# A graph layer's edge pass on one core: gathers issued ahead, scatters one pair closer, eight degree products and the inverse roots moved to its end

## The chip, the cores and the metric

The kernel runs on 1 core of one Trainium2 chip. The time is device microseconds of one execution, as a median over runs; the trace comes from one execution taken by the hardware profiler. PE is TensorE, DVE is VectorE, ACT is ScalarE, POOL is GpSimd, and SP issues DMAs only.

## The reference

Two layers over 50,000 nodes with 256 features and 12,500 edges sorted by destination. In the first layer h is the relu of the layer norm of x; each edge gathers the rows of its two ends, normalises them, projects them to q, k and v, forms a message and adds it to the row of its destination. The second layer is a weighted, symmetrically normalised graph convolution (with self loops) and a two-layer head.

```python
h = jnp.maximum(_layernorm(x), 0.0)
# first layer, per edge
dk = silu(edge_attr @ Wdk.T + bdk); dv = silu(edge_attr @ Wdv.T + bdv)
attn = silu(jnp.sum(q[dst] * k[src] * dk, axis=1)) * cosine_cutoff(edge_weight)
msg = v[src] * dv * attn[:, None]
agg = segment_sum(msg, dst, N)
x = x + h + agg @ Wo.T + bo
# second layer, h taken anew from x; row = src, col = dst
deg = segment_sum(edge_weight, row, N) + 1.0
dinv = where(deg > 0, rsqrt(deg), 0.0)
h7 = segment_sum((h @ W)[col_sl] * norm[:, None], row_sl, N) + b   # norm = dinv[row] * ew * dinv[col]
x = x + relu(h7 @ W1 + b1) @ W2 + b2
```

## The kernel before

The edges lie in 98 columns of 128 (`EC`), two columns to a pair, so 49 pairs (`EP`). There are three stages.

**Edge pass of the first layer (the function `messages` of each engine, steps 0 to 55).** Each engine has its own instruction list, written out in the order of steps; step s works on several pairs at once, each at another lag. At step s POOL gathers the four blocks of pair s (rows of x, 128 x 256 each: two by source into `XS`, a ring of two pairs, two by destination into `kept`, which has a place for every column; both count into `m_x`), DVE takes the statistics of pair s-1, ACT makes its relu, POOL takes the inverse roots of pair s-2 (`power`), and PE projects pair s-4 (`project`), merges the messages of pair s-5 by destination and multiplies those of pair s-6 by Wo. ACT copies that product out at step k+7 for pair k, and POOL adds it to the table `sums0` in DRAM (`scatter_add`) at step k+9 (`SCATTER_LAG`), after a wait for the scatter of the pair before. POOL's list is fully written out: up to step 10 `power` stands ahead of the scatter, from step 11 behind it. Before the first scatter POOL waits until SP's 98 fills of `sums0` with the row bo have landed (`s_fill`). The engines read each other's progress by semaphores only; there is no scheduler.

**Degrees.** The degree of every node is one sum of 98 products on PE (`hot`): DVE writes two one-hot matrices for each column of edges (a 128 x 128 and a 128 x 392), PE multiplies them into bank 7. `HOT_STEPS` says how many belong to each of the first ten steps, six buffers deep. `degrees` (three DVE instructions) at step 10, a square root on ACT at step 11 and `inverse_roots` (seven linked DVE instructions) at step 12 turn the sum into the table `dinv`.

**SP's queue.** SP first issues the 98 fills of `sums0`, 512 KB each. Behind them, from step 4 on, it fills the second table `sums1` with zeros, two fills (1 MB) to a step. From step 10 on it also loads each pair's attributes and destinations, and waits for PE's progress there.

**Second layer over edges, by quads of columns (`messages2`), then the nodes (`nodes`).** A quad's first two inputs are the look-up of `dinv` (DVE one-hot `HT`, PE product `n_look`, DVE selection) and a gather from `sums0`, which waits for all scatters of the first stage. Then come count, add, statistics, relu, a product on PE and a scatter into `sums1`. The last stage goes over the nodes in 98 groups of 512.

## Time and profile before

| | us |
|---|---|
| median of 3 runs (lowest to highest) | 1797.54 (1796.07 to 1799.05) |
| the profiled execution | 1786.2 |
| span of its trace | 1784.6 |
| PE busy over the span | 1600.9 (90%) |
| DVE busy | 1419.5 (80%) |
| POOL busy | 1196.1 (67%) |
| ACT busy | 1126.8 (63%) |

The shares of busy time are means over the three stages. The edge pass ends at about 660 us of the span, the quads at about 995 us, and the nodes take the rest. A busy PE in this profile has modelled ends, so the distance from one instruction's start to the next like it says more than a duration. In rows of a timeline the bracket says how long the engine stood idle before the row and what ended that.

### The profile page before, as it was taken

Reading aid. Unit: us, or ns where it says so; the run is one execution under the profiler, and the core shown is the slowest. Engines: PE = TensorE matmul, PEld = TensorE weight load, DVE = VectorE, ACT = ScalarE, POOL = GpSimd, SP = SyncE. Lnnn points to the kernel's source line nnn. Section 1 sums busy time; section 2 is a strip of 40 time slices with the busy share of each in tenths; the row PEclk is TensorE's granted clock in tenths of the full one; section 3 lists DMA queues with packets and bytes.
Section 4 is the critical chain, followed back from the end, with each engine's and each line's share of the span. In section 5 each row is a group of like instructions: output and inputs, shape, how many; then the busy total and the mean of one; then the engine's idle time right before and its main releaser. Section 6 shows DMA issues by size and latency. Waiting matters only on the chain.

```text
span 1784.6 us, 28458 instructions
## 1 busy us (share of the span) xinstructions
PE 1600.9 (90%) x6406; PEld 1092.2 (61%) x6406; DVE 1419.5 (80%) x5671; ACT 1126.8 (63%) x2148; POOL 1196.1 (67%) x854
## 2 busy tenths in 40 slices
PE   6999999999999937676655499999999999999998
PEld 3566666666666625454444267666766766666676
DVE  8887877777777629998888488888888888888873
ACT  2344666666666512232233498989888898898884
POOL 5324888888888457888887666666666666666650
PEclk9999999999999978888887699999999999999999
DMA  9999666666666735667666799999999999999971
GB/s 370 417 416 360 164 186 184 187 192 194 191 185 185 235 56 129 138 138 148 135 147 97 183 246 268 269 270 274 268 265 268 269 272 262 266 270 264 273 218 79
DMA packets 148036, 398.79 MB, mean 223 GB/s; under 512 B 20144, under 2 KB 56756, under 8 KB 147974
## 3 DMA queue, kind: packets, MB, share of 16 engines
q1 hardware_dynamic: 88038, 278.61, 44.9%
q0 software_dynamic: 56416, 115.46, 34.4%
q10 hardware_dynamic: 3520, 4.07, 0.7%
q14 instruction: 45, 0.37, 0.1%
q8 instruction: 17, 0.28, 0.1%
HBM read 217.84 MB, written 180.23 MB: 223 GB/s over the span
## 4 chain that ended last, share of the span: by engine, by line
PE 45%; POOL 22%; DVE 12%; DMA 12%; issue 6%; SPq 1%; ACT 1%; POOLq 0%; DVEq 0%; ACTq 0%
DMA out_dram<-cg 8%; PE bank L1324 8%; PE bank L1440 7%; PE bank L1429 7%; POOL sums_dram L522 6%; POOL kept L617 6%; PE bank L1317 4%; PE bank L1366 4%; PE bank L1331 4%; POOL b_rs L518 4%; DVE cg L1033 3%; POOL cg L526 2%; PE bank L1263 2%; PE bank L1305 2%; PE bank L1393 2%
## 5 line engine op out<-in xcount | busy, mean ns | idle before, releaser
L1429 PE MATMUL bank<-kept,w 128*128 128x512 f32 x784 | 354.3, 595 | 0.0
L1440 PE MATMUL bank<-w_sb,kept 128*128 128x256 f32 x1568 | 354.3, 379 | 0.0
L1440 PEld LDWEIGHTS bank<-w_sb,kept 128*128 128x128 f32 x1568 | 297.9, 190 | 81.9 <-issue 46.4
L617 POOL TENSOR_TENSOR kept<-kept 128x1024 f32<-128x1024 f32 x94 | 223.1, 2373 | 177.2 <-DVE cg L1033 177.2
L1393 PE MATMUL bank<-cg,en 128*128 128x256 f32 x386 | 124.7, 465 | 123.3 <-ACT cg L1188 73.8
L1429 PEld LDWEIGHTS bank<-kept,w 128*128 128x128 f32 x784 | 142.1, 191 | 141.7 <-issue 141.7
L518 POOL TENSOR_TENSOR b_rs<-b_ve,minus_half 128x8 f32<-128x8 f32 x96 | 199.2, 2075 | 21.3 <-DVE b_ve L1050 21.3
L1216 ACT ACTIVATE kept<-kept,b_nb,b_rs 128x256 f32<-128x256 f32 x392 | 202.2, 589 | 0.7 <-DVE b_nb L1023 0.7
L1226 ACT ACTIVATE kept<-kept,b_nb,b_rs 128x256 f32<-128x256 f32 x392 | 202.2, 589 | 0.0
L522 POOL DMA_INDIRECT sums_dram<-ub,sidx x96 | 156.8, 1633 | 53.5 <-issue 26.5
L1063 DVE SCALAR_TENSOR_TENSOR kept<-cg,dinv,kept 128x256 f32<-128x256 f32 x392 | 165.7, 484 | 27.0 <-DMA cg<-sums_dram 21.9
L1324 PE MATMUL bank<-qkv_w,zT 128*128 128x512 f32 x392 | 184.8, 593 | 0.1
L1393 PEld LDWEIGHTS bank<-cg,en 128*128 128x128 f32 x386 | 88.4, 236 | 153.5 <-issue 138.4
L1101 ACT ACTIVATE zT<-bank 128x512 f32<-128x512 f32 x98 | 58.5, 597 | 176.1 <-PE bank L1305 174.9
L1207 ACT ACTIVATE kept<-bank 128x1024 f32<-128x1024 f32 x98 | 100.4, 1024 | 104.7 <-PE bank L1419 104.7
L1033 DVE TENSOR_TENSOR cg<-kept,bank 128x1024 f32<-128x1024 f32 x98 | 119.5, 1220 | 40.3 <-PE bank L1440 33.4
L1038 DVE BATCH_NORM_STATS2 b_st<-kept 128x6 f32<-128x256 f32 x392 | 137.0, 412 | 1.7 <-DMA kept<-in_x_dram 1.7
L619 POOL DMA_DIRECT2D kept<-sums_dram x98 | 92.2, 941 | 65.9 <-POOL kept L617 63.0
L1042 DVE BATCH_NORM_STATS2 b_st<-kept 128x6 f32<-128x256 f32 x392 | 136.1, 410 | 0.0
L1324 PEld LDWEIGHTS bank<-qkv_w,zT 128*128 128x128 f32 x392 | 73.5, 189 | 95.6 <-issue 92.0
L564 POOL TENSOR_TENSOR rs<-ve,minus_half 128x6 f32<-128x6 f32 x49 | 69.0, 1408 | 93.1 <-DVE ve L851 85.9
L1241 ACT ACTIVATE kept<-bank,b_col 128x512 f32<-128x512 f32 x196 | 122.2, 673 | 11.4 <-PE bank L1429 11.3
(188 smaller groups left out, 3332.2 us busy)
## 6 DMA issues: line engine op xcount, KB each, us to landing
sums_dram<-cg SPq DMA_DIRECT2D x196, 512.0 KB, 4.8
kept<-in_x_dram SPq DMA_DIRECT2D x97, 512.0 KB, 5.9
kept<-sums_dram POOLq DMA_DIRECT2D x97, 512.0 KB, 9.9
cg<-sums_dram SPq DMA_DIRECT2D x97, 512.0 KB, 8.6
out_dram<-cg SPq DMA_DIRECT2D x97, 512.0 KB, 9.8
row_k<-keys_dram SPq DMA_DIRECT2D x24, 256.0 KB, 4.5
row_s<-in_src_dram SPq DMA_DIRECT2D x24, 256.0 KB, 4.1
row_d<-in_dst_dram SPq DMA_DIRECT2D x41, 128.0 KB, 3.5
```

Source lines behind the costliest of these rows:

```text
L518: pool.tensor_tensor(to, var, minus_half[:, 0:width].rearrange("p (a b) -> p a b", b=1), ALU.pow).then_inc(done, 1)
L522: pool.indirect_dma_start(sums, bass.IndirectOffsetOnAxis(idx, 0), rows, None, bounds_check=bound, compute_op=ALU.add).then_inc(done, 16)
L617: pool.tensor_tensor(X1[k.slot(8)], X[k.slot(4)], H[k.slot(2)], ALU.add).then_inc(g_xh, 1)
L1033: dve.tensor_tensor(OUT[k.slot(2)], X1[k.slot(8)], bank[:, to:to + 2, :].rearrange("p a b -> p (a b)"), ALU.add).then_inc(g_fin, 1)
L1038: ins = dve.bn_stats(b_st[a.slot(2)][:, j, :], X[a.slot(4)][:, j * D:(j + 1) * D])
L1063: ins = dve.scalar_tensor_tensor(AG[k.slot(2)][:, at0], S1[k.slot(4)][:, at0], dinv[:, bass.ds(k.value(0, G) + j, 1)], H1[k.slot(2)][:, at ...
L1216: ins = act.activation(H1[k.slot(2)][:, j * D:(j + 1) * D], X1[k.slot(8)][:, j * D:(j + 1) * D], ACT.Relu, bias=b_nb[k.back(-4).slot(2)][: ...
L1226: ins = act.activation(H[k.slot(2)][:, j * D:(j + 1) * D], X[k.slot(4)][:, j * D:(j + 1) * D], ACT.Relu, bias=b_nb[k.slot(2)][:, j, :], sc ...
L1324: ins = pe.matmul(bank[:, 2 + i, :], zT[i][:, c, :], qkv_w[:, c, D:3 * D], start=(c == 0), stop=(c == KC - 1))
L1393: ins = pe.matmul(bank[:, 6 * q + to // 2, (to % 2) * D:(to % 2 + 1) * D], EN[q][i][:, to * P:(to + 1) * P], H1e[q][:, i, :], start=(i == to),
L1429: ins = pe.matmul(bank[:, 2 + m, :], w01[:, c, m * P:(m + 1) * P], hT[k.slot(2)][:, c * GN:(c + 1) * GN], start=(c == 0), stop=(c == KC - 1))
L1440: ins = pe.matmul(to, rT[k.slot(2)][:, c * GN + j * P:c * GN + (j + 1) * P], w2_sb[:, c, :], start=False, stop=(c == KC - 1), skip_group_c ...
```

## The change

- Gathers: those by destination for pairs 10 to 18 are issued by POOL in steps 4 to 8, two pairs to a step, behind `power`, and count into a semaphore of their own (`m_ahead`). In steps 10 to 18 POOL gathers only by source. DVE waits for the two kinds apart, which splits its loop into two loops.
- Scatters: at step 14 POOL scatters two pairs instead of one, so that from then on pair k is scattered at step k+8, and the stage has 57 steps on POOL instead of 58.
- Degrees: steps 4 to 9 hold 56 of the products instead of 64. The last eight stand behind the last pair, two buffers deep, followed there by `degrees`, the square root and `inverse_roots`. The buffers lie in `CG[0]` and `CG[1]`, and the gather of the third quad waits for the inverse roots, because it writes over them.
- Fills of `sums1`: three to a step in steps 10 to 41 and two at the end, instead of two to a step in steps 4 to 52.
- Two loads of the last stage (w2, 256 KB, and the rows b2, 512 KB) are issued by ACT at step 14 instead of at the start.

```diff
@@ -30,11 +30,15 @@
 FRONT_FROM = 4
 QUAD_LAG = 3
 FRONT_AT = (7, 10, 13, 16, 19, 22)
-HOT_STEPS = (10, 8, 8, 8, 11, 11, 11, 11, 10, 10)
+HOT_STEPS = (10, 8, 8, 8, 10, 10, 9, 9, 9, 9)
+HOT_EARLY = sum(HOT_STEPS)
 HOT_RING = 6
+HOT_LATE_RING = 2
 SCATTER_LAG = 9
+CATCH_UP = (14,)
 POWER_FIRST = 11
 LOADED = 10
+AHEAD_FROM, AHEAD_TO, AHEAD_STEP = 10, 19, 2
 CUTOFF = 5.0
 EPS = 1e-5
 PI = 3.14159265358979
...
@@ -229,6 +229,12 @@
 
 
         XS = [CG[1][:, i // 2, i % 2 * D:(i % 2 + 1) * D] for i in range(4)]
+        late_a = CG[1][:, 2:4, :].rearrange("p a d -> p (a d)")
+        late_p = [late_a[:, 2 * COLS:2 * COLS + P], rows_b[:, 2 * COLS:2 * COLS + P]]
+        late_c = [late_a[:, i * COLS:(i + 1) * COLS] for i in range(HOT_LATE_RING)]
+        deg1, root = [rows_b[:, i * COLS:(i + 1) * COLS] for i in range(2)]
+        some, turn = late_c
+
         G2 = [CG[2][:, i, :].rearrange("p (a d) -> p a d", a=2) for i in range(4)]
         Z2 = ring("z2_", 2, [P, 2, D])
...
-
-            def load_edges(s):
-                if s.past(LOADED):
-                    load_pair(sp, s)
-
-                k = s.back(LATER)
-                if k.within(EP):
-
-                    for i in range(2):
-                        sp.dma_start(sums1[bass.ds(k.value(0, 2 * GN) + i * GN, GN), :]
-                                     .rearrange("(p j) d -> p (j d)", j=G), rows_0).then_inc(s_fill1, 16)
+            def fill_sums1(at, count):
+
+                for i in range(count):
+                    sp.dma_start(sums1[bass.ds(at + i * GN, GN), :].rearrange("(p j) d -> p (j d)", j=G),
...
             sp.wait_ge(s_zero, 1)
             for i in range(1, Q):
                 sp.dma_start(sums1[N + i * SPARE:N + i * SPARE + P, :], rows_0[:, 0:D]).then_inc(s_fill1, 16)
-            run_steps(sp, EP, LATER, 2, LOADED - LATER, load_edges, start=LATER)
+            assert LOADED % 2 == 0
+            full = NG // 3 // 2 * 2
+            with sp.Fori(LOADED // 2, (LOADED + full) // 2) as reg:
+                for u in range(2):
+                    s = Step(u, reg, 2)
+                    load_pair(sp, s)
+                    fill_sums1(s.value(-LOADED, 3 * GN), 3)
+            fill_sums1(full * 3 * GN, NG - full * 3)
...
@@ -532,7 +540,18 @@
                     pool.wait_ge(m_h, p - 1)
                 for k in (2 * p, 2 * p + 1):
                     gather(XS[k % 4], x, node_i[:, k, 1:2], last_node, m_x[p % 2])
-                    gather(kept[:, k, :], x, node_i[:, k, 0:1], last_node, m_x[p % 2])
+                    if not AHEAD_FROM <= p < AHEAD_TO:
+                        gather(kept[:, k, :], x, node_i[:, k, 0:1], last_node, m_k[p % 2])
+
+            def gather_ahead(p):
+
+                first = AHEAD_FROM + AHEAD_STEP * (p - 4)
+                for k in range(2 * first, 2 * min(first + AHEAD_STEP, AHEAD_TO)):
+                    gather(kept[:, k, :], x, node_i[:, k, 0:1], last_node, m_ahead)
+
+            def scattered(p):
+
+                return min(EP, max(0, p - SCATTER_LAG + sum(p > c for c in CATCH_UP)))
 
             def messages(p):
 
@@ -540,8 +559,9 @@
                     gather_x(p)
                 if p < POWER_FIRST:
                     power(p - 2)
-                k = p - SCATTER_LAG
-                if 0 <= k < EP:
+                if 4 <= p < AHEAD_FROM:
+                    gather_ahead(p)
+                for k in range(scattered(p), scattered(p + 1)):
                     pool.wait_ge(m_UB, k + 1)
                     pool.wait_ge(m_idx, k + 1)
                     if k >= 1:
...
@@ -580,7 +600,7 @@
                 pool.sem_inc(s_edges)
 
             pool.wait_ge(s_ends, 16)
-            for p in range(EP + SCATTER_LAG):
+            for p in range(EP + SCATTER_LAG - len(CATCH_UP)):
                 if p == 2:
...
@@ -592,6 +612,8 @@
                 if p < NQ:
                     if p >= 3:
                         pool.wait_ge(n_x1, Q * (p - 2))
+                    elif p == 2:
+                        pool.wait_ge(s_tab_sb, 1)
...
+                q = k % HOT_LATE_RING
+                if k >= HOT_EARLY + HOT_LATE_RING:
+
+                    dve.wait_ge(s_hotmm, k - HOT_LATE_RING + 1)
+                dve.tensor_scalar(late_p[q], iota_p, pkey[:, k:k + 1], ew_f[:, k:k + 1], ALU.is_equal, ALU.mult)
+                dve.tensor_scalar(late_c[q], iota_c[:, :], ckey[:, k:k + 1, 1], None, ALU.is_equal).then_inc(s_hot, 1)
 
             def cosine():
 
...
                 if a.within(EP):
                     q = a.slot(2)
-                    dve.wait_ge(m_x[q], a.turns(2, 64))
+                    dve.wait_ge(m_x[q], a.turns(2, 32))
                     for i in range(2):
                         dve.bn_stats(st1[q][:, 0, i, :], XS[2 * q + i])
+                    if late or a.reg is None and a.off >= AHEAD_TO:
+
+                        dve.wait_ge(m_k[q], a.turns(2, 32, 1 - len(range(AHEAD_FROM + q, AHEAD_TO, 2))))
+                    elif a.reg is None and a.off < AHEAD_FROM:
+                        dve.wait_ge(m_k[q], a.turns(2, 32))
+                    else:
+                        dve.wait_ge(m_ahead, 32 * (AHEAD_TO - AHEAD_FROM))
...
-                if s.reg is None and s.off == len(HOT_STEPS):
+                if s.reg is None and s.off == EP + MESSAGE_STEPS - 1:
+                    dve.wait_ge(s_fill, 16 * (NG + 1))
+                    for j in range(HOT_EARLY, EC):
+                        late_hot(j)
                     degrees()
-                if s.reg is None and s.off == len(HOT_STEPS) + 2:
                     inverse_roots()
 
-            run_steps(dve, EP, MESSAGE_STEPS, 2, 6, messages)
+            assert AHEAD_FROM % 2 == 0 and AHEAD_TO % 2 == 1 and MESSAGE_STEPS + 6 < AHEAD_TO
+            static = (MESSAGE_STEPS + 7) // 2
+            for k in range(2 * static):
+                messages(Step(k))
+            with dve.Fori(static, (AHEAD_TO + 1) // 2) as reg:
+                for u in range(2):
+                    messages(Step(u, reg, 2))
+            with dve.Fori((AHEAD_TO + 1) // 2, (EP - 1) // 2) as reg:
+                for u in range(2):
+                    messages(Step(u, reg, 2), late=True)
+            for k in range((EP - 1) // 2 * 2, EP + MESSAGE_STEPS):
+                messages(Step(k))
...
-            for t, w in ((w_t, w_in), (w1_raw, w1_in), (wo_t, wo_in), (w2_sb, w2_in)):
+            for t, w in ((w_t, w_in), (w1_raw, w1_in), (wo_t, wo_in)):
                 act.dma_start(t[:, :, :], w.rearrange("(c p) k -> p c k", p=P)).then_inc(s_ldw, 16)
-            act.dma_start(b2_rows[:, :], b2.rearrange("(a d) -> a d", a=1).broadcast_to([P, G * D])).then_inc(s_b2, 16)
...
-                if s.reg is None and s.off == len(HOT_STEPS) + 1:
-                    act.wait_ge(s_deg, 1)
-                    act.activation(root[:, :], deg1[:, :], ACT.Sqrt).then_inc(s_rsq, 1)
-
+                if s.reg is None and s.off == LOADED + 4:
+                    act.dma_start(w2_sb[:, :, :], w2_in.rearrange("(c p) k -> p c k", p=P)).then_inc(s_b2, 16)
+                    act.dma_start(b2_rows[:, :], b2.rearrange("(a d) -> a d", a=1).broadcast_to([P, G * D])
+                                  ).then_inc(s_b2, 16)
...
             run_steps(act, EP, MESSAGE_STEPS, 4, 9, messages)
+
+            act.wait_ge(s_deg, 1)
+            act.activation(root, deg1, ACT.Sqrt).then_inc(s_rsq, 1)
...
             def hot(k):
                 pe.wait_ge(s_hot, k + 1)
-                pe.matmul(bank[:, 7, 0:COLS], hot_p[k % HOT_RING][:, :], hot_c[k % HOT_RING][:, :], start=k == 0,
-                          stop=k == EC - 1).then_inc(s_hotmm, 1)
+                if k < HOT_EARLY:
+                    of_p, of_c = hot_p[k % HOT_RING][:, :], hot_c[k % HOT_RING][:, :]
+                else:
+                    of_p, of_c = late_p[k % HOT_LATE_RING], late_c[k % HOT_LATE_RING]
+                pe.matmul(bank[:, 7, 0:COLS], of_p, of_c, start=k == 0, stop=k == EC - 1).then_inc(s_hotmm, 1)
 
...
@@ -1353,6 +1408,9 @@
                     project(1)
                 if s.reg is None and s.off >= 2:
                     for k in hots(s.off):
+                        hot(k)
+                if s.reg is None and s.off == EP + MESSAGE_STEPS - 1:
+                    for k in range(HOT_EARLY, EC):
                         hot(k)
                 if t.within(EP):
```

On POOL at steps 4 and 9 (L526 is a gather, L522 a scatter, L564 `power`; `cg_1` holds the rows by source, `kept` those by destination). Before, from `power` of step 5 to that of step 6, and then from the last `power` ahead of the fills on:

```order
L564 TENSOR_TENSOR rs_1<-ve_1,minus_half 128x6
L526 DMA cg_1<-in_x_dram,node_i 128x256
L526 DMA kept<-in_x_dram,node_i 128x256
L526 DMA cg_1<-in_x_dram,node_i 128x256
L526 DMA kept<-in_x_dram,node_i 128x256
L564 TENSOR_TENSOR rs_0<-ve_0,minus_half 128x6
...
L564 TENSOR_TENSOR rs_1<-ve_1,minus_half 128x6
L522 DMA sums0_dram<-ub4,sidx 50304x256 x2
L526 DMA cg_1<-in_x_dram,node_i 128x256
L526 DMA kept<-in_x_dram,node_i 128x256
L526 DMA cg_1<-in_x_dram,node_i 128x256
L526 DMA kept<-in_x_dram,node_i 128x256
```

The same two places now (L534 is the gather, L530 the scatter, L584 `power`):

```order
L584 TENSOR_TENSOR rs_1<-ve_1,minus_half 128x6
L534 DMA kept<-in_x_dram,node_i 128x256 x4
L534 DMA cg_1<-in_x_dram,node_i 128x256
L534 DMA kept<-in_x_dram,node_i 128x256
L534 DMA cg_1<-in_x_dram,node_i 128x256
L534 DMA kept<-in_x_dram,node_i 128x256
L584 TENSOR_TENSOR rs_0<-ve_0,minus_half 128x6
...
L584 TENSOR_TENSOR rs_1<-ve_1,minus_half 128x6
L530 DMA sums0_dram<-ub4,sidx 50304x256 x2
L534 DMA cg_1<-in_x_dram,node_i 128x256 x2
L584 TENSOR_TENSOR rs_0<-ve_0,minus_half 128x6
```

Four gathers more stand between two `power` in steps 4 to 7 (two more in step 8), and behind the first scatter only the two gathers by source are left.

On POOL at step 14, now (`row_k_1`, `row_s_0` and `row_s_1` are buffers of messages for pairs 5, 6 and 7); before, every step from 11 on has four gathers, one row of two scatters and one `power`:

```order
L534 DMA cg_1<-in_x_dram,node_i 128x256 x2
L530 DMA sums0_dram<-row_k_1,sidx 50304x256 x2
L530 DMA sums0_dram<-row_s_0,sidx 50304x256 x2
L584 TENSOR_TENSOR rs_0<-ve_0,minus_half 128x6
L534 DMA cg_1<-in_x_dram,node_i 128x256 x2
L530 DMA sums0_dram<-row_s_1,sidx 50304x256 x2
```

The scatter of pair 6, which waits for that of pair 5, has moved ahead of the `power` of step 14.

On DVE at the end of the edge pass, before (L767 writes the last message, L908 is `HT`, L898 the selections of quad 0, L924 its first add), and now (L803, L958, L948 and L974 are the same four; L689 and L690 make one product's one-hot matrices, L738 to L740 are `degrees`, L745 to L751 `inverse_roots`):

```order
L767 SCALAR_TENSOR_TENSOR msg_1<-bank,aa_0,ds_1 128x256
L908 TENSOR_SCALAR z2_0<-row_k_0,part_f 128x512
L898 SCALAR_TENSOR_TENSOR cg_0,found<-iota_c,ckey,bank 128x392 x4
L908 TENSOR_SCALAR z2_1<-row_k_1,part_f 128x512
L916 SCALAR_TENSOR_TENSOR ds_0,cnt2_0<-row_s_0,src_f,earlier 128x128
L916 SCALAR_TENSOR_TENSOR ds_1,cnt2_0<-row_s_0,src_f,earlier 128x256
L924 TENSOR_TENSOR kept<-kept,cg_1 128x256
```

```order
L803 SCALAR_TENSOR_TENSOR msg_1<-bank,aa_0,ds_1 128x256
L689 TENSOR_SCALAR cg_1<-iota_c,pkey,ew_f 128x128
L690 TENSOR_SCALAR cg_1<-iota_c,ckey 128x392
...
L738 TENSOR_SCALAR cg_0<-bank 128x392
...
L745 RECIPROCAL cg_0<-cg_0 128x392
...
L751 TENSOR_TENSOR dinv2<-dinv 128x392
L958 TENSOR_SCALAR z2_0<-row_k_0,part_f 128x512
L948 SCALAR_TENSOR_TENSOR cg_0,found<-iota_c,ckey,bank 128x392 x4
```

Twenty-six instructions have come to stand between the last message and `HT`.

## Rows read from the trace of the kernel before

**Rows 1.** Window: length, busy us (count) by engine, PEclk, DMA share, GB/s.
```profile
200.00:527.00 327.00, 326.98 (x1454) 224.69 (x1455) 257.85 (x1216) 213.84 (x484) 271.02 (x213) 1.00 0.67 187
```
**Rows 2.** Timeline of PE: start us, us, engine, line, operation [idle before <-releaser].
```profile
118.19 3.56 PE L1263 MATMUL bank<-kept 128*128 128x392 f32 x10 [0.53 <-DVE kept L661]
...
175.51 0.49 PE L1347 MATMUL bank<-eq,msg 128*128 128x128 f32 x2
...
200.02 0.49 PE L1347 MATMUL bank<-eq,msg 128*128 128x128 f32 x2 [2.59 <-DVE msg L767]
...
605.92 1.89 PE L1366 MATMUL bank<-wo_t,stt 128*128 128x256 f32 x8
...
616.75 1.89 PE L1366 MATMUL bank<-wo_t,stt 128*128 128x256 f32 x8
```
**Rows 3.** Timeline of POOL in the start, at the fills' end and beside the roots.
```profile
98.73 1.42 POOL L564 TENSOR_TENSOR rs<-ve,minus_half 128x6 f32<-128x6 f32 x1 [10.57 <-DVE ve L851]
...
159.87 1.67 POOL L522 DMA_INDIRECT sums_dram<-ub,sidx  x1 [3.77 <-DMA sums_dram<-cg]
...
167.80 1.17 POOL L526 DMA_INDIRECT kept<-in_x_dram,node_i  x1 [0.30 <-issue]
...
192.13 1.62 POOL L522 DMA_INDIRECT sums_dram<-en,sidx  x1 [0.31 <-DVE ve L851]
```
**Rows 4.** Timeline of DVE, steps 9 to 13 and one of the steady steps.
```profile
149.25 0.33 DVE L660 TENSOR_SCALAR kept<-kept,ew_f 128x128 f32<-128x128 f16 x1
...
149.83 0.34 DVE L660 TENSOR_SCALAR kept<-kept,ew_f 128x128 f32<-128x128 f16 x1
...
169.65 0.56 DVE L709 TENSOR_SCALAR kept<-bank 128x392 f32<-128x392 f32 x1
...
173.47 0.75 DVE L741 BATCH_NORM_STATS2 st<-cg 128x6 f32<-128x256 f32 x2 [2.46 <-DMA kept<-in_x_dram,node_i]
...
192.07 2.60 DVE L716 RECIPROCAL kept<-kept 128x392 f32<-128x392 f32 x1
...
197.99 0.74 DVE L741 BATCH_NORM_STATS2 st<-cg 128x6 f32<-128x256 f32 x2
...
296.46 0.42 DVE L751 TENSOR_TENSOR kd<-bank,ds 128x256 f32<-128x256 f32 x1 [1.50 <-PE bank L1324]
```
**Rows 5.** DMA queue of the gathers, 100 to 158 us: packets, MB, share.
```profile
q0 software_dynamic: 576, 1.57, 6.8%
```
**Rows 6.** Timeline of SP's queue: the fills of sums1 that wait for nothing.
```profile
150.50 13.72 SPq L417 DMA_DIRECT2D sums_dram<-cg  x12
...
604.27 11.23 SPq L417 DMA_DIRECT2D sums_dram<-cg  x10
```
**Rows 7.** Timeline of POOL at the end of the edge pass.
```profile
608.00 1.60 POOL L522 DMA_INDIRECT sums_dram<-en,sidx  x1 [0.20 <-issue]
...
618.78 1.55 POOL L522 DMA_INDIRECT sums_dram<-en,sidx  x1 [7.32 <-DMA sums_dram<-en,sidx]
...
647.73 1.55 POOL L522 DMA_INDIRECT sums_dram<-en,sidx  x1 [2.87 <-DMA sums_dram<-en,sidx]
...
654.20 1.55 POOL L522 DMA_INDIRECT sums_dram<-ub,sidx  x1 [3.05 <-DMA sums_dram<-en,sidx]
...
660.12 1.10 POOL L526 DMA_INDIRECT cg<-sums_dram,node_i  x1 [2.50 <-DMA sums_dram<-ub,sidx]
```
**Rows 8.** Timeline of PE at the end of the edge pass.
```profile
632.89 1.96 PE L1366 MATMUL bank<-wo_t,stt 128*128 128x256 f32 x8 [0.78 <-ACT en L1119]
...
641.36 4.59 PE L1382 MATMUL bank<-dinv,z 128*128 128x392 f32 x8 [2.75 <-DVE z L908]
```
**Rows 9.** Timeline of ACT there.
```profile
629.07 0.60 ACT L1119 ACTIVATE en<-bank 128x512 f32<-128x512 f32 x1 [1.06 <-PE bank L1366]
```
**Rows 10.** Timeline of DVE there.
```profile
638.65 0.62 DVE L898 SCALAR_TENSOR_TENSOR cg<-iota_c,ckey,bank 128x392 f32<-128x392 f16 x1 [9.21 <-PE bank L1382]
...
663.03 0.42 DVE L924 TENSOR_TENSOR kept<-kept,cg 128x256 f32<-128x256 f32 x1 [21.05 <-DMA cg<-sums_dram,node_i]
```

More of the change, by code:

```diff
@@ L201, in build @@
         iota_c = sb("iota_c", [P, COLS], F16)
-        iota_p = temp([P, P], F16)
+        iota_p = iota_c[:, 0:P]
         iota_i = temp([P, COLS], I32)
-        deg1 = temp([P, COLS])
-        root = temp([P, COLS])
-        turn = temp([P, COLS])
-        some = temp([P, COLS])
         dinv = sb("dinv", [P, COLS])
@@ L432, in _ @@
                 sp.dma_start(sums1[N + i * SPARE:N + i * SPARE + P, :], rows_0[:, 0:D]).then_inc(s_fill1, 16)
-            run_steps(sp, EP, LATER, 2, LOADED - LATER, load_edges, start=LATER)
+            assert LOADED % 2 == 0
[6 more added lines that the diff above has]
+            fill_sums1(full * 3 * GN, NG - full * 3)
+            for k in range(LOADED + full, EP):
+                load_pair(sp, Step(k))
             def load_src(s):
@@ L708, in degrees @@
                 dve.wait_ge(s_hotmm, EC)
[L709 to L711 removed]
+                link(dve.tensor_scalar(deg1, bank[:, 7, 0:COLS], 1.0, None, ALU.add))
+                link(dve.tensor_scalar(some, deg1, 0.0, None, ALU.is_gt))
+                dve.tensor_scalar(deg1, deg1, 1e-30, None, ALU.max).then_inc(s_deg, 1)
             def inverse_roots():
                 dve.wait_ge(s_rsq, 1)
[L716 to L721 removed]
+                link(dve.reciprocal(root, root))
+                link(dve.tensor_tensor(turn, root, root, ALU.mult))
+                link(dve.tensor_tensor(turn, turn, deg1, ALU.mult))
+                link(dve.tensor_scalar(turn, turn, -0.5, 1.5, ALU.mult, ALU.add))
+                link(dve.tensor_tensor(root, root, turn, ALU.mult))
+                link(dve.tensor_tensor(dinv[:, :], root, some, ALU.mult))
                 dve.tensor_tensor(dinv2[:, :], dinv[:, :], dinv[:, :], ALU.mult).then_inc(s_tab_sb, 1)
@@ L1268, in _ @@
                     hot(k)
-            pe.wait_ge(s_ldw, 96)
+            pe.wait_ge(s_ldw, 80)
             pe.wait_ge(s_const, 10)
```

27 lines of the change are left out of this document (9 added, 18 removed).

## The prediction

> **What bounds the kernel now.** I read the windows first, then the timelines of PE and POOL through the edge pass, and last all five queues between 600 and 670 us. In the windows the reader sees a stage in which PE never rests: 326.98 of 327 us, with POOL at 271 [rows 1]. The timeline of PE gives the length of a steady step, 616.75 - 605.92 = 10.83 us from one product with Wo to the next [rows 2]. So within the steady steps nothing can be won by freeing POOL or DVE; only PE's own work and the places where PE stands still count. Three such places are in reach.
>
> First, the start. Steps 4 to 9 carry 64 degree products beside the pairs; ten PE instructions, two to a product, take 3.56 us, so 0.7 us a product, and behind the sixth PE waits 0.53 us for DVE [rows 2]. Second, steps 10 to 13. POOL waits for the fills of `sums0` until 159.87 [rows 3], its gathers for pair 10 are late, DVE stands 2.46 us until 173.47 [rows 4], and two steps on, DVE's inverse roots (192.07 to 197.99) let PE stand 2.59 us at 200.02 [rows 2, 4]. Third, the end. PE ends its last pair at 632.89 + 1.96 = 634.85, which I call T [rows 8]. POOL is by then several scatters behind: each waits for the one before, the last starts at 654.20, and the first gather of the next stage at 660.12 [rows 7]. DVE stands 21.05 us and adds the first gathered rows at 663.03 = T + 28.2 [rows 10].
>
> **The start, part by part.** Eight products fewer in steps 4 to 9 take 8 x 0.7 = 5.6 us from PE. They don't arrive, since step 11 needs pair 10's rows by source, which POOL still gathers only behind the first scatter, and that waits for the fills. When do the fills end now? Eighteen gathers are new ahead of their end. Twelve gathers in the 58 us of [rows 5] took 1.57 MB and 6.8% of the DMA time, 0.33 us each, with the queues full; 18 x 0.33 = 5.9 us. The two loads that leave the start are 768 KB, six gathers' worth, 2.0 us. The fills' end moves from 159.87 to about 163.8. From there: two scatters at 1.62 + 0.31, 3.86 us [rows 3]; two gathers instead of four at 1.10 [rows 7] and 0.30 for the issue, 2.8 us; the landing. Bounds for the landing: before it was 173.47 - 168.97 = 4.5 us after the last issue's end [rows 3, 4], among twelve fills of `sums1` that stood in SP's queue from 150.50 on [rows 6] and are now gone; at the end of the pass, with the queues near empty, 2.9 us pass from a gather's start to the add of its rows [rows 7, 10], 1.8 from its issue's end. I take 2.6, nearer the lower end, since the fills among which the longer one was measured are gone, while two scatters still lie ahead in the same queue. Sum: 163.8 + 3.86 + 2.8 + 2.6 = 173.1, so DVE goes on 0.4 us sooner than before. On POOL itself the gathers ahead cost nothing: four at 1.4 are 5.6 us a step in steps 4 to 7, where it waits 10.57 us for DVE's `ve` [rows 3]. If that cover were short, pair 5's to 8's own gathers, which stand behind them, would be late, and the fills' end would hide that in turn, for it holds POOL anyway.
>
> After that the two steps to PE's next merge took 200.02 - 175.51 = 24.51 us, of which 2 x 10.83 = 21.66 are PE's work; the 2.85 us between go with the roots [rows 2]. By itself POOL would have been the next to be late there, with four gathers, two scatters and `power` filling its step; two gathers fewer give it 2.8 us a step to spare in steps 10 to 18.
>
> The second scatter at step 14 costs POOL 6.5 us in one step (647.73 to 654.20 is one with its wait [rows 7]). It has 2.8 spare in that step, so `power` comes up to 3.7 us late. Bounds 0 and 3.7 us for PE; I take 0.3, since DVE still waits 1.50 us for PE in a steady step [rows 4]. So T moves by -0.4 - 2.85 + 0.3 = -3.0 us.
>
> **The end, part by part.** POOL scatters pair 43 at 608.00, where 42 stood. Before, the next waited 7.32 us [rows 7], for ten fills of `sums1` went out at 604.27 with nothing to wait for [rows 6]; now all fills are out by step 42. So the scatters follow at 6.47 us: 614.5, 620.9, then pair 46 not before ACT has copied it (629.07 + 0.60 [rows 9]), 629.7, and 636.2, 642.6. The next gather starts 660.12 - 654.20 = 5.92 later, at 648.6 = T + 13.7, against T + 25.3. Its rows could be added at T + 16.6.
>
> But the way to that add now has the degrees in it. DVE can prepare two products, then waits for PE to end pair 48 at T. From there two buffers bind: DVE 0.58 us to write (149.83 - 149.25 [rows 4]), PE 0.7 to multiply, and twice a hand-over, for which no row here has this pattern; the bounds are PE alone, 0.7 us a product, and all in a row, 1.7. I take 0.95, nearer PE's, as two run at a time: T + 0.7 + 6 x 0.95 = T + 6.4. (What hides the first two is PE's last pair.) Then `degrees`, 1.4 us (169.65 until the idle time of 2.46 before 173.47 begins), the square root with its hand-over 0.9 (an estimate, 392 elements like DVE's row at 169.65 with 0.56, and two hand-overs), `inverse_roots` 5.9 (192.07 to 197.99 [rows 4]), `HT` 0.5, PE's look-up 4.6 as at 641.36, where PE had stood before it, too [rows 8]; four selections at 0.62, a little overlapped, 2.3 [rows 10]; the second `HT` and two counts 1.0 (estimated from the same row: 512, 128 and 256 elements against 392 in 0.62). Together T + 23.0 for the add, against T + 28.2: 5.2 us sooner. DVE's list decides now and no longer POOL, with 6.4 us between them. POOL's third round of gathers waits for the roots at T + 14.7, and comes to it later than that.
>
> Sum: -3.0 - 5.2 = -8.2 us, in the profiled execution 1786.2 to 1778.0. The runs of before have their median 11.3 us above that execution; I take the difference on to it: 1797.5 - 8.2 = 1789.3.
>
> **A rule against it.** Beside the last scatters POOL now has DVE's products and roots. A scatter that ran beside the reciprocal took 1.62 us, the last one, with DVE idle, 1.55 [rows 3, 7], so I charge nothing. The Trainium skill (SBUF — State Buffer, "Who interferes with whom") says otherwise: VectorE and GpSimd share a pair of ports that the first to come holds for its whole instruction, and copies and tensor_scalar in the two-port modes, or two SBUF inputs against a reading GpSimd, shut the other out; its section "SBUF: two separate sides" adds that GpSimd then can't write DMA descriptors. No run here shows it so far.
>
> **The rivals.**
> 1. The fills end no later than before (POOL's gathers find room in the queues). For it: the span of 58 us at 6.8% is only one stretch, and POOL's own waits of 10.57 us show nothing of the queues [rows 3, 5]. Against: the fills that follow those of `sums0` went out at 150.50 without a wait, so the queues are never short of work [rows 6]. Then 3.9 us more of the products arrive: -12.1, 1785.4.
> 2. The end brings nothing. As a mechanism here: DVE's eight products (4.7 us), `degrees` (1.4) and roots (5.9) hold POOL off for their 12 us, and its first gather goes to T + 25.7; or each product costs 1.7 and the look-up comes as late. Then only the start's 3.0 is left: 1794.5. The rule above gives this. Against it: the 1.62 us.
> 3. Slower. Three fills to a step, 1.5 MB instead of 1, in steps 10 to 41, onto a DMA share of 0.67 [rows 1]. From step 19 on POOL gathers four blocks again, and they must land within a step. If they come late, 23 steps grow. The third fill has the bytes of four gathers, so 4 x 0.33 = 1.3 us of the queues. From 8.2 / 23 = 0.36 us a step on, the change is slower than before; at 0.5 it is 11.5 - 8.2 = +3.3, 1800.8. Against it: the 1.50 us by which DVE waits for PE must be used up first [rows 4], and the fills go out ahead of the gathers, not among them.
> 4. The step 14 scatter pushes PE by its full 3.7: -4.8, 1792.7.
>
> **How the numbers follow.** Forecast 0.46; rival 1 0.18; rival 2 0.15; rival 3 0.13; rival 4 0.08. Without the rule rival 2 had 0.11. By 0.2% I mean 3.6 us, about what a measurement of this kernel can tell. Faster: the forecast and rival 1 whole but for 0.02, rival 4 for the most part and half of rival 2 make 0.74; within 0.2%: the other half and the small ends of the others, 0.14; slower 0.12. The forecast's own range is 1786 to 1792.5. With rival 1's lower end and rival 2, and part of rival 3, 1782 to 1799 leaves out some 2 in 10.
>
> **What would show it.** POOL's first scatter at about 164 rather than 160; PE without a gap over 1 us from step 12 on; T about 3 us earlier; scatters at the end 6.5 us apart and the first gather of quads about T + 14; the add of its rows about T + 23, with DVE busy or waiting for PE ahead of it and not for a DMA. It would be wrong if PE's steps 19 to 41 were over 10.9 us, if the last eight products took over 10 us, or if the node stage, which nothing here touches, moved by more than 3 us.

## The result, and the profile after

| | before | after |
|---|---|---|
| median of 18 runs each, us | 1800.34 | 1794.47 |
| lowest run, us | 1793.90 | 1791.18 |
| the profiled execution's span, us | 1784.6 | 1792.9 |

The ratio of after to before is 0.997, with a 95% interval of 0.9962 to 0.9979: 5.9 us faster by the medians, where 8.2 were forecast. The time lies in the predicted range. One of the 18 runs of before took 3376.35 us; without it the median is 1800.30. But the two traces differ by 8.3 us the other way. The execution of before from which the prediction was read was shorter than any of the 18 timed runs; the first experiment takes a second trace of before.

I follow four marks through a trace: M_k, the start of the product that ends PE's merge of pair k (0.11 us into the second L1404 row of a pair, L1349 before); T, the end of PE's last pair; and the add of the first gathered rows (DVE, L974 in after, L924 before).

| us | M0 | M6 | M9 | M16 | M44 | T | add |
|---|---|---|---|---|---|---|---|
| before, first trace | 73.9 | 176.8 | 212.2 | 288.0 | 591.1 | 634.9 | T + 28.2 |
| after | 71.4 | 182.5 | 214.9 | 290.7 | 600.3 | 644.1 | T + 23.3 |

The windows of after (PE busy, weight loads, DVE, ACT, POOL, then granted clock, DMA share, GB/s):

```profile
50.00:100.00 50.00, 43.04 (x148) 24.25 (x147) 37.22 (x157) 20.30 (x44) 21.28 (x20) 0.96 1.03 413
100.00:150.00 50.00, 45.25 (x162) 27.91 (x161) 33.86 (x147) 15.72 (x35) 25.11 (x23) 0.94 1.03 412
150.00:200.00 50.00, 49.47 (x211) 32.99 (x211) 38.47 (x178) 28.43 (x64) 28.19 (x22) 1.00 0.53 138
```

PE has eight products fewer in the first two windows and still stands 7.0 and 4.8 us. From 150 on it hardly stands at all, where it had lost 2.6 us to the roots before [rows 2]. The end of the edge pass, POOL first, then PE and DVE:

```profile
606.41 1.60 POOL L530 DMA_INDIRECT sums_dram<-en,sidx  x1 [0.19 <-issue]
617.24 1.59 POOL L530 DMA_INDIRECT sums_dram<-en,sidx  x1 [0.20 <-issue]
623.59 1.54 POOL L530 DMA_INDIRECT sums_dram<-ub,sidx  x1 [2.90 <-DMA sums_dram<-en,sidx]
...
652.65 1.55 POOL L530 DMA_INDIRECT sums_dram<-ub,sidx  x1 [3.01 <-DMA sums_dram<-en,sidx]
...
658.48 1.46 POOL L534 DMA_INDIRECT cg<-sums_dram,node_i  x1 [2.43 <-DMA sums_dram<-ub,sidx]
```
```profile
642.14 1.97 PE L1424 MATMUL bank<-wo_t,stt 128*128 128x256 f32 x8 [0.78 <-ACT en L1168]
643.94 3.18 PE L1319 MATMUL bank<-cg 128*128 128x392 f32 x8
...
649.37 1.58 PE L1319 MATMUL bank<-cg 128*128 128x392 f32 x4 [0.27 <-DVE cg L690]
659.50 4.43 PE L1440 MATMUL bank<-dinv,z 128*128 128x392 f32 x8 [8.55 <-DVE z L958]
```
```profile
650.99 0.57 DVE L738 TENSOR_SCALAR cg<-bank 128x392 f32<-128x392 f32 x1 [1.09 <-PE bank L1319]
...
658.88 0.48 DVE L958 TENSOR_SCALAR z<-row_k,part_f 128x512 f32<-128x512 f32 x1
663.98 0.62 DVE L948 SCALAR_TENSOR_TENSOR cg<-iota_c,ckey,bank 128x392 f32<-128x392 f16 x1 [4.62 <-PE bank L1440]
...
667.38 0.41 DVE L974 TENSOR_TENSOR kept<-kept,cg 128x256 f32<-128x256 f32 x1
```

T is 642.14 + 1.97 = 644.11. The late products end at T + 6.8, POOL's first gather starts at T + 14.4, the add at T + 23.3: DVE's list now sets the end, no longer POOL [rows 7, 10]. At the start DVE, ACT and PE wait in a way that the trace of before does not have at all. Here is step 4 as the changed kernel's second trace has it (below, e1), POOL, PE, DVE and ACT:

```profile
64.56 1.08 POOL L534 DMA_INDIRECT kept<-in_x_dram,node_i  x1
...
73.94 1.01 POOL L534 DMA_INDIRECT kept<-in_x_dram,node_i  x1 [0.30 <-issue]
```
```profile
71.81 0.39 PE L1404 MATMUL bank<-eq,msg 128*128 128x128 f32 x2
...
74.61 1.03 PE L1386 MATMUL bank<-qkv_w,zT 128*128 128x256 f32 x4
78.68 4.22 PE L1319 MATMUL bank<-kept 128*128 128x392 f32 x12 [3.04 <-DVE kept L682]
```
```profile
72.33 0.14 DVE L798 TENSOR_TENSOR aa<-sa,cut 128x1 f32<-128x1 f32 x1
76.25 0.48 DVE L803 SCALAR_TENSOR_TENSOR msg<-bank,aa,ds 128x256 f32<-128x256 f32 x1 [3.78 <-remote]
```
```profile
76.22 0.60 ACT L1175 ACTIVATE ds<-bank 128x512 f32<-128x512 f32 x1 [2.68 <-remote]
```

The message at L803 waits for the merge, which PE's rows have ended at 72.2. DVE goes on at 76.25, ACT, which waits for another product of PE, at 76.22. "remote" is what the page calls another core or an unknown queue: the profile can name nobody. In the semaphore events of the trace the merge's signal comes 4.0 us after its modelled end, and three later signals of PE within 0.2 us of it. I call this a late signal. DVE goes on 1.3 us after the end of POOL's row of eight gathers (73.94 + 1.01); in all such waits of steps 4 to 7, here and in e11, it is 1.15 to 1.36 us. The step is then 20.4 us long, where it was 17.2.

Behind the edge pass the two traces differ as well. From POOL's last scatter of the quads to the end, 790.1 us pass before and 794.2 after (789.8 and 792.9 in e0 and e1), though the change leaves the node stage as it was. The prediction had called a move of over 3 us there a sign of being wrong.

### The profile page after: what moved, and what is told of

The parts are those of the page before. It is cut to its first block, busy times and chain, and to the rows that moved or that the text cites. A ratio compares the mean times of both kernels' runs of the same rounds, so it can differ in the third digit from the quotient of the medians.

```text
span 1792.9 us, 28468 instructions
## 1 busy us (share of the span) xinstructions
PE 1613.1 (90%) x6406; PEld 1093.8 (61%) x6406; DVE 1411.9 (79%) x5670; ACT 1126.5 (63%) x2146; POOL 1192.4 (67%) x854
## 4 chain that ended last, share of the span: by engine, by line
PE 46%; POOL 20%; DVE 15%; issue 7%; DMA 7%; ACT 2%; another core or an unknown queue 2%; SPq 1%; POOLq 0%; DVEq 0%; ACTq 0%
PE bank L1498 8%; PE bank L1487 8%; PE bank L1379 8%; POOL sums_dram L530 6%; POOL kept L639 6%; DMA out_dram<-cg 5%; POOL b_rs L526 4%; PE bank L1424 4%; PE bank L1372 4%; PE bank L1386 4%; DVE cg L1083 3%; POOL cg L534 2%; PE bank L1319 2%; PE bank L1477 2%; PE bank L1360 2%
## 5 line engine op out<-in xcount | busy, mean ns | idle before, releaser
L526 POOL TENSOR_TENSOR b_rs<-b_ve,minus_half 128x8 f32<-128x8 f32 x96 | 200.5, 2088 | 21.9 <-DVE b_ve L1100 21.9
L530 POOL DMA_INDIRECT sums_dram<-ub,sidx x96 | 154.6, 1611 | 52.7 <-issue 28.1
L584 POOL TENSOR_TENSOR rs<-ve,minus_half 128x6 f32<-128x6 f32 x49 | 71.1, 1451 | 103.9 <-DVE ve L887 80.4
L1477 PE MATMUL bank<-identity,kept 128*128 128x128 f32 x784 | 104.0, 276 | 29.1 <-DVE kept L1113 29.1
```

The costliest lines, as they stand in the source:

```text
L526: pool.tensor_tensor(to, var, minus_half[:, 0:width].rearrange("p (a b) -> p a b", b=1), ALU.pow).then_inc(done, 1)
L530: pool.indirect_dma_start(sums, bass.IndirectOffsetOnAxis(idx, 0), rows, None, bounds_check=bound, compute_op=ALU.add).then_inc(done, 16)
L1477: ins = pe.transpose(bank[:, c, j * P:(j + 1) * P], AG[k.slot(2)][:, j * D + c * P:j * D + (c + 1) * P], identity[:, :])
```

## The experiments

Ratios are to before, timed on the same chip. There were three chips: e0 to e3 ran on one on which before has a median of 1813.5, e4 to e7 on one where it has 1800.7, e8 to e11 on one where it has 1800.5. All columns but the ratio come from one trace each, and those of e3, e4, e5, e8 and e9 are of the fastest of their runs: the ratios and medians count, and the traces say where.

| | M6 | M9 | M16 | M16 to M44, a step | T | add - T | span | ratio (95%) |
|---|---|---|---|---|---|---|---|---|
| e0 before | 179.2 | 218.4 | 297.4 | 11.45 | 661.9 | 28.3 | 1813.3 | - |
| e1 after | 183.1 | 215.6 | 292.1 | 11.41 | 655.5 | 23.4 | 1801.3 | 0.994 (0.9919 to 0.9961) |
| e2 none ahead | 170.4 | 207.5 | 294.6 | 11.46 | 659.1 | 23.4 | 1810.1 | 0.9965 (0.9947 to 0.9984) |
| e3 two fills | 181.9 | 214.4 | 291.2 | 11.32 | 651.9 | 24.2 | 1800.2 | 0.9958 (0.9944 to 0.9973) |
| e4 five pairs ahead | 171.3 | 203.8 | 284.1 | 11.08 | 638.1 | 23.0 | 1780.8 | 0.991 (0.989 to 0.993) |
| e5 none ahead, no second scatter | 170.0 | 206.6 | 283.7 | 11.10 | 638.1 | 22.9 | 1785.2 | 0.9939 (0.9919 to 0.9959) |
| e6 fills last | 183.1 | 215.5 | 291.3 | 11.18 | 648.1 | - | - | - |
| e7 late products only | 175.6 | 209.6 | 287.5 | 11.00 | 639.2 | 28.9 | 1795.6 | 0.9993 (0.9976 to 1.0009) |
| e8 e4, no second scatter | 171.4 | 203.8 | 280.1 | 11.12 | 635.1 | 23.5 | 1778.1 | 0.9915 (0.9892 to 0.9937) |
| e9 e4, second scatter at 12 | 171.2 | 206.1 | 284.6 | 11.10 | 639.1 | 23.9 | 1784.1 | 0.993 (0.9916 to 0.9945) |
| e10 two rows | 175.8 | 209.4 | 285.2 | 11.10 | 639.6 | 23.5 | 1787.5 | 0.9931 (0.9915 to 0.9946) |
| e11 after | 182.7 | 215.2 | 291.0 | 11.17 | 647.4 | 23.2 | 1793.3 | 0.9965 (0.9951 to 0.9978) |

**e0: before, traced again** (no edit).

> The kernel before, profiled a second time. Its first profiled execution was 14 us shorter than the median of its runs. Theory A (the edge pass is the same in every execution, and the executions differ in the node stage, which nothing here touches): PE's steps are 10.83 us again, the merge of pair 6 starts at 176.8 and T (end of PE's last pair) is 634.9, each within 1 us, and the span is 1785 to 1800 with the difference behind 1000 us. Theory B (the edge pass varies too, with PE's results signalled late in some executions, whatever the kernel): T is 3 to 9 us later, and part of what the first comparison charged to the change is chance.

Theory B, and more than it expected: T is 27 us later. The window from 300 to 580 (PE busy first; in the first trace PE was busy throughout [rows 1]), and one of its steps, POOL and DVE:

```profile
300.00:580.00 280.00, 271.58 (x1173) 179.88 (x1172) 200.76 (x980) 173.94 (x394) 214.24 (x172) 1.00 0.64 177
```
```profile
306.90 1.13 POOL L526 DMA_INDIRECT cg<-in_x_dram,node_i  x1 [0.20 <-issue]
...
311.00 1.01 POOL L526 DMA_INDIRECT kept<-in_x_dram,node_i  x1 [0.30 <-issue]
312.31 1.62 POOL L522 DMA_INDIRECT sums_dram<-ub,sidx  x1 [0.30 <-issue]
```
```profile
310.15 0.16 DVE L762 TENSOR_TENSOR aa<-sa,cut 128x1 f32<-128x1 f32 x1
311.98 0.48 DVE L767 SCALAR_TENSOR_TENSOR msg<-bank,aa,ds 128x256 f32<-128x256 f32 x1 [1.67 <-remote]
```

PE is not always busy in the steady steps, and DVE waits for the merge until POOL's fourth gather is issued (311.00 + 1.01). All twelve traces of these experiments and that of after have such late signals in the steady steps; the first trace of before alone has none, and exactly 10.83 us a step. The one run of e0, 1814.9 us, fits the median of 1813.5 on its chip, so I take a trace with late signals for the ordinary one.

**e1: after, traced again** (no edit).

> The changed kernel again. Theory A (what its first trace shows is its own: the start loses 5.6 us to pair 6, the steps with three fills and four gathers lose 6.5 us): the merge of pair 6 is at 182.5 and T at 644, each within 1 us. Theory B (late signals are a matter of the execution): T anywhere from 632 to 644, and the merge of pair 6 moves by over 2 us. In the time both expect 0.997 of before (1794).

The start is as in the first trace of after (M6 at 183.1), so it is the change's own. T isn't: theory A fails there, and at 655.5 it lies outside theory B's range, too. The ratio, 0.994, is below the 0.997 that both expected. As for T, the steps from pair 16 on vary by chip and execution (11.06 in the first trace of after, 11.41 here, 11.17 in e11). Against e0, on one chip, the change does this:

| us | start to M6 | M6 to M9 | M9 to M16 | M16 to T | T to add | the rest | sum |
|---|---|---|---|---|---|---|---|
| forecast | -0.4 | -2.85 | +0.3 | 0 | -5.2 | 0 | -8.2 |
| e1 less e0 | +3.9 | -6.7 | -2.5 | -1.1 | -4.9 | -0.8 | -12.0 |

**e2: without gathers ahead.**

```diff
-                    if not AHEAD_FROM <= p < AHEAD_TO:
-                        gather(kept[:, k, :], x, node_i[:, k, 0:1], last_node, m_k[p % 2])
+                    gather(kept[:, k, :], x, node_i[:, k, 0:1], last_node, m_k[p % 2])
...
-                if 4 <= p < AHEAD_FROM:
-                    gather_ahead(p)
```

> The changed kernel without the gathers ahead: pairs 10 to 18 are gathered in their own steps; all else stays. Theory A (eight gathers a step beside full queues made steps 4 to 8 20.3 us long): those steps go back to 17.2 to 18.9 less 0.7 us for each product left out, so the merges of pairs 0 to 4 come 5 to 9 us sooner than in the changed kernel; behind them four gathers, the scatter and the fills' end hold POOL again, so that 3 to 8 us of it arrive at T: ratio to before 0.993 to 0.996. Theory C (the start is held by something else in the change, such as the distribution of the products): the merges of pairs 0 to 4 stay within 1 us of the changed kernel, and the time is the changed kernel's or up to 5 us above it: 0.997 to 1.000.

Theory A, and more than it expected: the first four steps are 16.6 and three times 17.6 us instead of 20.4 to 21.3, and no late signal stands in them. M6 is 12.7 us sooner. But the step from M10 to M11 takes 19.9 us: POOL scatters twice there and waits 6.76 us for a scatter to land, PE then 4.18 us. So the median is 4.6 us above e1's, and the ratio just above theory A's range. POOL and PE there:

```profile
211.18 1.57 POOL L530 DMA_INDIRECT sums_dram<-row_k,sidx  x1 [0.31 <-issue]
219.51 1.56 POOL L530 DMA_INDIRECT sums_dram<-row_s,sidx  x1 [6.76 <-DMA sums_dram<-row_k,sidx]
```
```profile
225.33 2.08 PE L1377 MATMUL bank<-qkv_w,zT 128*128 128x256 f32 x4 [4.18 <-DVE at L783]
```

**e3: two fills a step**, as before, from step 4 on.

```diff
-                    fill_sums1(s.value(-LOADED, 3 * GN), 3)
...
+                k = s.back(LATER)
+                if k.within(EP):
+                    fill_sums1(k.value(0, 2 * GN), 2)
```

> The changed kernel with the fills of sums1 as before: two to a step from step 4 on, ten at once at the end. Theory A (the third fill beside four gathers made steps 20 to 48 0.23 us longer, 6.5 us in all): all steps from pair 9 on are 10.83 us, T is 6.5 us sooner; the ten fills hold the last scatters 7 us, but the list of DVE hides most of that, so the add of the first gathered rows comes 0 to 2 us later against T: 4.5 to 6.5 us sooner in all, ratio 0.9935 to 0.9945. Theory B (those steps vary by the execution): T within 1 us of the changed kernel, and the end 0 to 2 us later: 0.997 to 0.998.

Neither: the steps from M16 on stay at 11.32 us, with late signals, and T is 3.6 us sooner, within what steps vary by. The median is 2.1 us above e1's, and the intervals overlap: no difference is measured.

**e4: one pair ahead a step** (10 to 14).

```diff
-AHEAD_FROM, AHEAD_TO, AHEAD_STEP = 10, 19, 2
+AHEAD_FROM, AHEAD_TO, AHEAD_STEP = 10, 15, 1
```

> The changed kernel with one pair gathered ahead in each of steps 4 to 8 (pairs 10 to 14) instead of two pairs a step (10 to 18): six gathers a step for eight. Theory A (the more gathers POOL issues in a row, the longer DVE and ACT wait for PE's products that its records show as ended): the merges of pairs 0 to 4 are 18 to 19.5 us apart, between the 17.6 without gathers ahead and the 20.4 with four more; pairs 15 to 18 lose 0.5 us each again; if the second scatter at step 14 finds POOL full, 3 to 9 us more. Theory D (it is the DMA bytes ahead in the queues, not the row of gathers): the merges are 20 us apart until the last gather ahead. Ratio to before 0.990 to 0.995.

Theory A in kind, but under its 18 to 19.5 us: the steps are 17.5, 18.5 and three of 17.6, so that two of them cost 0.9 us each against e2, and the others nothing. DVE's wait for the merge is 0.8 us, twice, and has a name:

```profile
70.81 1.09 POOL L534 DMA_INDIRECT kept<-in_x_dram,node_i  x1 [0.30 <-issue]
```
```profile
72.86 0.48 DVE L803 SCALAR_TENSOR_TENSOR msg<-bank,aa,ds 128x256 f32<-128x256 f32 x1 [0.81 <-PE bank L1404]
```

POOL's row ends at 71.90, before the merge is awaited for long. The step with two scatters takes 13.54 us, 2.7 too many.

**e5: none ahead, one scatter at step 14** (e2's edit, and `CATCH_UP = ()`).

> Without the gathers ahead and without the second scatter at step 14; late products, late roots and three fills to a step stay. Theory A (without room on POOL the second scatter costs a whole step: 19.92 us between the merges of pairs 10 and 11 instead of 10.83 to 11.2): that step is 11.2 us, T is 8 to 9 us sooner than in the kernel without gathers ahead alone (659.1), about 650.5; the first gather of quads starts at T + 20 instead of 14, and DVE's list, not it, still sets the add at T + 23.4 to 25: ratio 0.990 to 0.993. Theory F (the long step is a mishap of one execution): T stays within 2 us of 659, ratio 0.996 to 0.998.

Theory A: the step of 19.9 us is 10.83, and the first gather at T + 19.4 still doesn't set the add (T + 22.9). The ratio, 0.9939, is a little above what was expected.

**e6: all fills behind the last loads.**

```diff
-                    fill_sums1(s.value(-LOADED, 3 * GN), 3)
-            fill_sums1(full * 3 * GN, NG - full * 3)
...
+            with sp.Fori(0, NG // 2) as reg:
+                fill_sums1(reg * (2 * GN), 2)
```

> The changed kernel with all fills of sums1 issued behind the last pair's loads, so that none runs beside the pairs from step 10 on; the quads wait for them, and the time as a whole says nothing. Theory A1 (PE's results come late only where four gathers and two scatters a step meet the fills): the merges of pairs 16 to 44 are 10.83 us apart, as in the first trace of before, and T is some 14 us sooner than 655.5 of the changed kernel on this chip. Theory A2 (the six indirect DMAs of a step do it by themselves): the steps stay at 11.0 to 12.1 us, 11.4 in the mean, and T within 2 us of 655.5. Steps 4 to 8, beside the fills of sums0, stay at 20.4 us by both.

Theory A2 in the steps: 11.18 us with no fill beside them, 40.8 us of late signals at L803 between 320 and 580. So the late signals don't need the fills; what the steps that have them share is their six indirect DMAs, four gathers and two scatters. That T would be within 2 us of 655.5 doesn't hold (648.1), but the other kernels of this chip have short T too.

**e7: only the late products and roots**; gathers, scatters and fills of `sums1` as before (e3's edit on e5), and the two loads issued late, as in after.

> As before in gathers, scatters and fills of sums1 (two to a step from step 4 on, ten at the end); new are the eight late products and the late roots alone. Theory A (the start gains 0.7 us for each product left out, the merge behind the roots its 2.9 to 4.8 us, nothing is lost): the merges of pairs 0 to 5 come 3.5 to 8 us sooner than before (75.8 to 167.2), T is 6 to 11 us sooner than 661.9, and the add of the first gathered rows is at T + 29 to 30, since the late scatters hold POOL as before: ratio 0.991 to 0.995. Theory G (the fills' end takes back what the start gains, as the prediction had it): T only 3 to 4 us sooner, ratio 0.997 to 0.999.

No change in the time: 0.9993, whose interval holds theory G's 0.997 to 0.999 in part and nothing of theory A's. The start brings its products' time up to M5 (158.4 against 165.3 in the first trace of before) and gives most of it back at M6 (175.6 against 176.8), where DVE waits for the gathers that stand behind the fills' end:

```profile
156.50 1.67 POOL L530 DMA_INDIRECT sums_dram<-ub,sidx  x1 [6.33 <-DMA sums_dram<-cg]
...
164.55 1.01 POOL L534 DMA_INDIRECT kept<-in_x_dram,node_i  x1 [0.30 <-issue]
```
```profile
170.54 0.75 DVE L767 BATCH_NORM_STATS2 st<-cg 128x6 f32<-128x256 f32 x2 [7.72 <-DMA cg<-in_x_dram,node_i]
```

That is theory G's way. The rows land 5.0 us after the last issue, 1.9 in e10, where no fills of `sums1` stand in the queue. And the end is POOL's again (T + 28.9). e5 differs only in the fills and is 9.4 us faster by the medians; in the traces 6.0 of it stand at the end.

**e8: e4 with one scatter at step 14** (`CATCH_UP = ()`).

> One pair ahead in each of steps 4 to 8, and no second scatter at step 14. Theory A (the second scatter costs where a step on POOL has no room: 13.54 us between the merges of pairs 10 and 11 with five pairs ahead, 10.83 with nine): that step is 10.83 to 11.0, T is 2.5 us sooner against the kernel with the second scatter, the first gather of quads is at T + 19.5 instead of 14.2, and DVE's list, not it, sets the add, so that 1.5 to 2.5 us are left: ratio to before 0.989 to 0.991. Theory H (the second scatter is worth more at the end than it costs at step 14): 1 to 3 us slower than with it, 0.992 to 0.993.

Theory A in the trace: no step over 11 us from M5 to M15, T 3.0 us sooner than in e4, add at T + 23.5. The ratio is above that forecast, 0.9915, and no different from e4's.

**e9: e4 with the second scatter at step 12** (`CATCH_UP = (12,)`).

> One pair ahead in each of steps 4 to 8, the second scatter at step 12 instead of 14. Theory A: at step 12 two steps with two gathers still follow, POOL catches up, and the step costs 0 to 1 us instead of 2.7; T + 23 for the add as before: ratio 0.989 to 0.991. Theory H' (a second scatter costs 2.7 us wherever it stands): the ratio of the kernel with it at 14, 0.991 to 0.992.

Nearer theory H', and worse than it: two steps of 13.3 and 12.4 us, 4.0 lost where H' had 2.7, and a ratio of 0.993 where it had 0.991 to 0.992.

**e10: nine pairs ahead, in rows of their own.**

```diff
                     gather_x(p)
+                if 4 <= p - 1 and AHEAD_FROM + AHEAD_STEP * (p - 5) < AHEAD_TO:
+                    pool.wait_ge(m_msg, 2 * (p - 4) + 1)
+                    gather_ahead(p - 1)
                 if p < POWER_FIRST:
```

> The changed kernel with all nine pairs gathered ahead, but POOL waits between the step's own four gathers and the four ahead until DVE has written the first message of the step: two rows of four instead of one of eight. Theory A (DVE and ACT go on only when POOL's row of DMA issues ends, 1.0 us behind its last one): the 3.5 us in which DVE waits for the merge go, steps 4 to 8 are 17.5 to 18.5 us instead of 20.4, the merge of pair 6 comes 8 to 12 us sooner than in the changed kernel, the second scatter stays free: ratio 0.989 to 0.991. Theory I (the number of gathers in a step counts, not how they stand): 20 us again, the changed kernel's ratio, 0.994 to 0.997. Theory J (the second row falls into the degree products and holds their signals instead): the steps are 19 to 20 us.

Theory A in the steps, to the digit of e2: 16.58 and four of 17.56 us, with as many gathers ahead as in after. POOL and DVE in step 4:

```profile
68.00 1.01 POOL L534 DMA_INDIRECT kept<-in_x_dram,node_i  x1 [0.30 <-issue]
72.55 1.01 POOL L534 DMA_INDIRECT kept<-in_x_dram,node_i  x1 [3.54 <-DVE msg L804]
```
```profile
71.80 0.48 DVE L804 SCALAR_TENSOR_TENSOR msg<-bank,aa,ds 128x256 f32<-128x256 f32 x1
```

The message is written without a wait, 4.5 us sooner than in e1. What comes next is what the prediction had: the fills' end at 163.03, and DVE waiting for pair 10's rows until 171.25:

```profile
163.03 1.67 POOL L530 DMA_INDIRECT sums_dram<-ub,sidx  x1 [13.08 <-DVE sidx L893]
...
168.28 1.05 POOL L534 DMA_INDIRECT cg<-in_x_dram,node_i  x1 [0.30 <-issue]
```
```profile
171.25 0.75 DVE L771 BATCH_NORM_STATS2 st<-cg 128x6 f32<-128x256 f32 x2 [8.65 <-DMA cg<-in_x_dram,node_i]
```

M6 is 6.9 us sooner than in e11, the median 5.6 us lower. Theory A had 8 to 12 us for M6 and 0.989 to 0.991 for the ratio, which is 0.9931: the fills' end keeps the rest. Theories I and J are out.

**e11: after, beside e8 to e10** (no edit).

> The changed kernel once more, on the chip of the three others, for comparison with them: steps 4 to 8 of 20.4 us, pairs 16 to 44 at 11.0 to 11.5 us, the add at T + 23.3, ratio 0.994 to 0.997.

As expected in the steps, the end and the ratio.

**The best.** e8 has 1783.1 us by the median where before has 1800.5 and after 1794.8 on the same chip; e4 has 1785.4 against 1800.7. e8 beats both kernels on one chip, and e4's ratio is the same. The traces overstate it: e8's ends 15.2 us before e11's, and 4.8 us of that lie behind the quads' last scatter, where the two kernels are alike (788.1 and 792.9 us). Over all the traces that part takes 788.1 to 797.6 us, and no run shows why; the 11.6 us between the medians agree with T, 12.3 us sooner.

## Why the prediction was right or wrong

**The failed step** is "On POOL itself the gathers ahead cost nothing". I had counted POOL's own time, 5.6 us a step in a wait of 10.57, and that was right: in after POOL still waits 8.2 us. What wasn't counted is what a row of eight does to others: DVE and ACT stand until it has ended, DVE 2.3 to 3.8 us in each of four steps. e2 shows the whole cost, 12.7 us at M6. The next sentence, that the fills' end would hide it "in turn", covers part of it: the fills' end binds in e10 and puts M6 at 175.8, some 5.5 us above e2. The rest isn't hidden: e11 against e10 on one chip, 6.9 us at M6 and 5.6 in the median. The forecast had M6 0.4 us sooner; e1 has it 3.9 us later than e0.

**The base.** "So within the steady steps nothing can be won by freeing POOL or DVE" rested on an execution without late signals [rows 1]. In the ordinary one a step with four gathers and two scatters takes 11.0 to 11.5 us, one with two of each 10.83 (pairs 9 to 15 in after, e1, e11). So the gathers ahead win there: -2.5 us from M9 to M16 on e1's chip, and 1.3 between e5 and e11, on two chips with one time of before. I had also added the 11.3 us between the profiled execution and the median as a constant; such late signals fall in part in steps that the change touches. The two errors have opposite signs, and what is left depends on the chip: 10.3 us faster by the medians of e1, 5.7 by e11's, 5.9 by the first. So it is in part luck that the time lies in the range.

**The fills' end.** Forecast 163.8, from +5.9 for 18 gathers and -2.0 for the two loads. Measured: 156.7 with no gathers ahead against 159.2 in e0, so -2.5; 163.03 in e10, so +6.3 for 18, 0.35 each against 0.33. That was right. The fills' end just doesn't bind in after, where POOL comes to the scatter at 163.3 by itself. The landing was 1.9 us, not 2.6 (e10).

**The roots.** 2.85 us forecast; M8 comes 10.83 us after M7 in after, 13.69 before: 2.86. With late signals it had been 15.62 in e0.

**The second scatter.** 0.3 forecast, bounds 0 and 3.7. It costs 0 with nine pairs ahead, 2.7 with five, 9.1 with none. For this change the small cost was right. For the others the bound of 3.7 was too low: it took the wait for the first scatter's landing from the end of the pass, 3.05 us with no gathers ahead of it [rows 7], where it was 4.28 us in e4 behind two gathers and 6.76 in e2 behind four.

**The end.** Forecast T + 23.0, measured T + 23.2 to 23.4; products T + 6.8 for 6.4; first gather T + 14.4 to 14.7 for 13.7. The gain is 4.9 us for 5.2. e5 and e8 show how much room there is: the first gather can come at T + 19.4 to 19.7, and the add stays at T + 22.9 and 23.5. Rival 2 is out. The rule beside it showed little: the two scatters that ran beside the reciprocal took 1.55 us each, and the first gather, beside the last of the roots, 1.46 instead of 1.10 us [rows 7]. Rival 1 is out by e10's fills, which end later than before. e7 shows the other side: with the fills of `sums1` as before, the late products and roots are worth nothing.

**Rival 3** had the right sign and place for the first trace of after (28 steps of 11.06, +6.5 us) and the wrong cause: e6 has no fills there and the same steps (11.18 us), and the ordinary before has them as well.

## What to carry to other kernels

Before reading a sum out of one profiled execution, hold its time against the runs: this one was shorter than all of them, and what it lacked, late signals, was what the change acted on. A wait that the profile can't name, on two engines at once, is worth a look at what POOL issues then. A few indirect DMAs moved ahead should stand as short rows with a wait between, placed so that no other engine waits for a merge meanwhile. Which of the two helps, the shorter row or the other place, e10 doesn't separate.
